# Two reciprocal roots of the Scan stage moved to GpSimd, and a group's sums and statistics spread over four rounds

## The reference

```
proj = hidden_states @ W_in.T                 # z (4096), xBC (4096 + 256), dt (64)
xBC  = silu(conv over 4 steps of xBC)         # x, B, C
dt   = softplus(dt + dt_bias)
y    = scan of x, B, C with decays exp(dt * A), + D * x
g    = y * silu(z)
gn   = g * rsqrt(mean(g * g) + 1e-5) * norm_w
out  = gn @ W_out.T                           # 4096 -> 256
```

## Time and profile before

| | us |
|---|---|
| median of 3 runs (3988.33 to 3993.56) | 3990.88 |
| the profiled execution | 3998.22 |
| its span | 3996.4 |
| TensorE busy in the span | 3464.1 (87%) |
| VectorE busy | 3056.8 (76%) |
| ScalarE busy | 1946.2 (49%) |
| GpSimd busy | 1167.3 (29%) |
| L3358, the taps, x408 | 302.4, 741 ns each |
| L3433, mE on GpSimd, x128 | 302.4, 2362 ns each |
| L3368, the scan, x128 | 297.1, 2321 ns each |

### The profile page before, as it was taken

The page is one execution under the profiler, slowest core; times in us unless marked ns, Lnnn a source line. Parts: engine busy times, 40 slices in busy tenths (PEclk is TensorE's granted clock), DMA queues, the critical chain, the costliest instruction groups (busy, mean ns, idle before and its releaser), DMA issues. The chain is left out here.

```text
span 3996.4 us, 65697 instructions
## 1 busy us (share of the span) xinstructions
PE 3464.1 (87%) x23619; PEld 2190.9 (55%) x23634; DVE 3056.8 (76%) x6556; ACT 1946.2 (49%) x4750; POOL 1167.3 (29%) x1208
## 2 busy tenths in 40 slices
PE   7799999999884485879899979889999999997875
PEld 3466666665553243654566655565655556564544
DVE  6799989989657766562477858869888888885678
ACT  4466666666553142421244434436655556563445
POOL 1533033306302100000011222106655555563210
PEclk9899999999997698989999989899999999997887
DMA  2222222222211100001000000311212222121000
GB/s 69 62 73 57 66 63 67 50 73 56 52 40 32 35 1 24 2 1 62 23 1 1 1 33 2 121 40 69 82 64 74 69 74 74 69 75 61 2 1 22
DMA packets 240529, 184.36 MB, mean 46 GB/s; under 512 B 117776, under 2 KB 216720, under 8 KB 239312
## 3 DMA queue, kind: packets, MB, share of 16 engines
q1 hardware_dynamic: 240208, 180.16, 15.0%
HBM read 164.88 MB, written 15.20 MB: 45 GB/s over the span
## 5 line engine op out<-in xcount | busy, mean ns | idle before, releaser
L310 PE MATMUL ps<-xT,min 128*128 128x512 f32 (+1 forms) x1072 | 505.1, 616 | 31.1 <-DVE macc L3358 30.8
L3358 DVE SCALAR_TENSOR_TENSOR macc<-ps,mcw,macc 128x508 f32<-128x508 f32 (+2 forms) x408 | 302.4, 741 | 82.7 <-ACT macc L3285 72.8
L3440 POOL TENSOR_TENSOR mSQ<-mSQ,mtn 128x512 f32<-128x512 f32 x128 | 239.9, 1874 | 365.7 <-ACT mtn L3310 365.6
L310 PEld LDWEIGHTS ps<-xT,min 128*128 128x128 f32 (+1 forms) x1072 | 192.3, 191 | 251.5 <-issue 204.8
L3433 POOL TENSOR_TENSOR mE<-mE,mCB 128x1024 f32<-128x1024 f32 x128 | 302.4, 2362 | 44.5 <-DVE mE L3368 26.5
L3368 DVE TENSOR_TENSOR_SCAN mE<-mE,mid 128x1024 f32<-128x1024 f32 x128 | 297.1, 2321 | 0.0
L3218 PE MATMUL ps<-mwo,macc 128*128 128x256 f32 x1024 | 245.0, 382 | 5.4 <-DVE macc L3375 5.4
L2946 ACT ACTIVATE hE<-ps 128x512 f32<-128x512 f32 x256 | 139.0, 595 | 220.9 <-PE ps L2908 220.9
L3306 ACT ACTIVATE mtn<-ps,mcol 128x64 f32<-128x64 f32 x1024 | 222.9, 334 | 3.0 <-PE ps L3197 2.8
L826 POOL TENSOR_TENSOR dTB<-did,dNB 128x1024 f32<-128x1024 f32 (+1 forms) x10 | 28.6, 2864 | 667.7 <-DMA dNB<-d_N 603.5
L2976 DVE TENSOR_REDUCE hMX<-ps 128x2 f32<-128x512 f32 x256 | 158.9, 684 | 60.0 <-PE ps L2887 60.0
(11 more groups left out here) (589 smaller groups left out, 8448.3 us busy)
## 6 DMA issues: line engine op xcount, KB each, us to landing
mE<-m_decay SPq DMA_DIRECT2D x128, 512.0 KB, 3.6
dwk<-in_L_attn_Wk SPq DMA_DIRECT2D x64, 128.0 KB, 2.3
dwq<-in_L_attn_Wq SPq DMA_DIRECT2D x64, 128.0 KB, 2.4
dwv<-in_L_attn_Wv SPq DMA_DIRECT2D x64, 128.0 KB, 2.4
dwg<-in_L_attn_Wg SPq DMA_DIRECT2D x64, 128.0 KB, 2.4
dwo<-in_L_attn_Wo SPq DMA_DIRECT2D x64, 128.0 KB, 2.7
min<-in_m_in SPq DMA_DIRECT2D x2, 4096.0 KB, 17.8
d_N<-dNT SPq DMA_DIRECT2D x256, 16.0 KB, 1.5
```

Source lines behind the costliest of these rows:

```text
L310: t = pe.matmul(out, w[:, j, :], self.c.xT[:, j, blk(g, 512)], start=j == 0, stop=j == 1)
L3358: x = dve.scalar_tensor_tensor(out=acc[:, :, 3 - j:T], in0=p[:, :, 0:T - 3 + j], scalar=self.cw[:, i, j:j + 1], in1=acc[:, :, 3 - j:T], op ...
L3440: pool.tensor_tensor(self.SQ[g % 2][:, :], self.SQ[g % 2][:, :], self.tn[s][:, :], ALU.add).then_inc(*self.sqa.up)
```

## The change

Both roots become a power with exponent -0.5 on GpSimd (`root_pool`); -0.5 stands in a constant of 128x4 in a spare column of `st`. The step "rsq" is now GpSimd's: it waits for `sw` and does one power. The step "rsqrt" is GpSimd's too: -mean, variance + 1e-5, the power, and the product. The one step "sums" becomes "sum0" to "sum3" with lags 7 to 10, and "stats" becomes "sta0" to "sta3" with lags 8 to 11 (the four aggregates go with "sta3"), one sum or statistic each. "rsqrt" and "scale" keep their lags 11 and 12, and "close" and "rsq" theirs. For the last group the steps stand together in three rounds of their own. The accumulator banks of a group come free with its last sum.

```
+    def root_pool(self, pool, own, out, var, eps, tmp):
+        if eps:
+            o = own(pool.tensor_scalar(tmp, var, eps, 1.0, ALU.add, ALU.mult))
+            pool.wait_ge(own.sem, o)
+        return pool.tensor_tensor(out, tmp, self.half, ALU.pow)
...
     def start_vector(self, dve, own):
         dve.memset(self.ones[:, :], 1.0)
+        dve.memset(self.half, -0.5)
...
-        for t in range(len(seq) + 13):
+        for t in range(len(seq) + 10):
...
-                            ("decay", t), ("rsq", t - 5), ("sums", t - 7), ("stats", t - 9), ("rsqrt", t - 11), ("scale", t - 12),
-                            ("tr", t - 1), ("taps", t), ("acc", t - 3), ("y", t - 2)):
+                            ("decay", t), ("rsq", t - 5), *self.ends(t), ("tr", t - 1), ("taps", t), ("acc", t - 3), ("y", t - 2)):
...
+    def ends(self, t):
+        last = len(self.seq) - 1
+        if t > last:
+            late = t - last
+            steps = {7: ("sum0", "sum1", "sum2", "sum3"), 8: ("sta0", "sta1", "sta2", "sta3", "rsqrt"), 9: ("scale",)}.get(late, ())
+            if steps:
+                return [(s, last) for s in steps]
+        steps = [(f"sum{j}", t - 7 - j) for j in range(4)] + [(f"sta{j}", t - 8 - j) for j in range(4)] + [("rsqrt", t - 11), ("scale", t - 12)]
+        return [(s, q) for s, q in steps if q < last]
...
-                    room[to] = room[to + 1] = self.summed.at(g + 1)
+                    room[to] = room[to + 1] = self.summed.at(4 * g + 4)
...
+            elif step[:3] == "sum":
+                j = int(step[3])
+                if j == 0:
+                    if g:
+                        dve.wait_ge(*c.xn.at(4 * self.n + g))
+                    dve.wait_ge(*self.accd.at(u + 1))
+                    dve.wait_ge(*self.rq.at(g + 1))
+                dve.scalar_tensor_tensor(out=c.R[:, j, :], in0=bank(to + j // 2)[:, blk(j % 2, 256)], scalar=self.sw[:, j:j + 1],
+                                         in1=c.X[:, 4 * g + j, :], op0=ALU.mult, op1=ALU.add).then_inc(*self.summed.up)
+            elif step[:3] == "sta":
+                j = int(step[3])
+                dve.wait_ge(*self.summed.at(4 * g + j + 1))
+                o = own(dve.bn_stats(c.st[:, j, 0:6], c.R[:, j, :]))
+                if j == 3:
+                    dve.wait_ge(own.sem, o)
+                    for k in range(4):
+                        x = dve.bn_aggr(c.st[:, k, 6:8], c.st[:, k, 0:6])
+                    x.then_inc(*self.var.up)
...
+            elif step == "rsq":
+                pool.wait_ge(*self.smv.at(g + 1))
+                c.root_pool(pool, own, self.sw[:, 0:4], None, 0, self.sw[:, 4:8]).then_inc(*self.rq.up)
+            elif step == "rsqrt":
+                flat = lambda k: c.st[:, :, k:k + 1].rearrange("p a b -> p (a b)")
+                pool.wait_ge(*self.var.at(g + 1))
+                pool.tensor_scalar(c.rsq[:, 12:16], flat(6), -1.0, 1.0, ALU.mult, ALU.mult)
+                o = own(c.root_pool(pool, own, c.rsq[:, 0:4], flat(7), 1e-5, c.pv))
+                pool.wait_ge(own.sem, o)
+                pool.tensor_tensor(c.rsq[:, 12:16], c.rsq[:, 12:16], c.rsq[:, 0:4], ALU.mult).then_inc(*self.off.up)
```

More of the change, by code:

```diff
@@ L84, in __init__ @@
         self.rsq = self.at("rsq", [128, 16], F32)
+        self.half, self.pv = self.st[:, :, 8:9].rearrange("p a b -> p (a b)"), self.rsq[:, 4:8]
         self.free0 = self.low
@@ L3108, in buffers @@
         self.dtx, self.sc, self.cols = v("dt_sum", 2), s("decay", 2), s("dt_cols", 2)
-        self.aexp, self.won, self.summed, self.smv, self.off = s("a", 2), p("wo", 2), v("summed", 4), v("mean", 4), v("offset", 4)
+        self.aexp, self.won, self.summed, self.smv, self.off = s("a", 2), p("wo", 2), v("summed", 16), v("mean", 4), p("offset", 4)
+        self.rq, self.var = p("rsqrt", 4), v("moments", 4)
         self.zm, self.xm, self.cbm, self.tr, self.y, self.accd, self.sm = (
@@ L3117, in ended @@
     def ended(self):
-        return self.summed.at(4)
+        return self.summed.at(16)
     def order(self):
         seq, units = self.seq, self.units_before
-        for t in range(len(seq) + 13):
+        for t in range(len(seq) + 10):
             for step, q in (("yd", t - 3), ("x2", t - 1), ("em", t - 1), ("z", t), ("sq", t - 3), ("x", t), ("close", t - 4), ("cb", t - 1),
-                            ("decay", t), ("rsq", t - 5), ("sums", t - 7), ("stats", t - 9), ("rsqrt", t - 11), ("scale", t - 12),
-                            ("tr", t - 1), ("taps", t), ("acc", t - 3), ("y", t - 2)):
+                            ("decay", t), ("rsq", t - 5), *self.ends(t), ("tr", t - 1), ("taps", t), ("acc", t - 3), ("y", t - 2)):
                 if not 0 <= q < len(seq):
@@ L3134, in order @@
                         yield step, q, units[q], g, i
-                elif step in ("close", "rsq", "sums", "stats", "rsqrt", "scale"):
+                elif step in ("close", "rsq", "rsqrt", "scale") or step[:3] in ("sum", "sta"):
                     if i == 31:
@@ L3378, in vector @@
                 dve.tensor_scalar(self.sw[:, 4:8], bank(6)[:, 0:4], 1.0 / 4096, 1e-5, ALU.mult, ALU.add).then_inc(*self.smv.up)
[L3379 to L3399, removed]
@@ L3401, in gpsimd @@
     def gpsimd(self, pool, own):
         c = self.c
+        pool.wait_ge(*c.const.at(1))
         pool.wait_ge(self.dma[0], 80)
```

## The result

The changed kernel takes 3958.92 us (median of 4 runs, 3955.16 to 3962.48), the kernel before 3989.61 in the runs beside it: 30.7 us less, a ratio of 0.9923 by the medians. The estimate of the ratio over the runs is 0.9917, with a 95% interval of 0.9903 to 0.9930, which is 28 to 39 us less. The forecast was 3957.8.

The account below looks back on a forecast made before the run. TensorE bounds Scan's rounds except at group ends, where late taps stall it. Loop -31.1 and tail -2.0 make -33.1 us: profiled 3998.2 becomes 3965.1, or 3957.8 with the 7.3 us distance to the median; likeliest case's range 3953 to 3963.

Parts of the forecast that it names:

- What stalls TensorE is the taps behind the roots: Scan's group ends: VectorE's roots, held by GpSimd, make the taps late for TensorE; moving both roots gives -31.1 us.
- Spreading is worth 0: VectorE in Scan: sums and statistics spread over rounds fit idle time and TensorE's slack, cost 0.
- P = 0.8 us: GpSimd at each root: assumed time of one 128x4 power, with bounds 0.258 and 2.36 us.
- The tail: 2.0 us less: Last group, all on the path: first root gains 1.3 us, second 0.7; bounds -3.1 to +1.1.
- Only the first power is long: Rival, GpSimd's first power: costs once what exceeds 3.6 us free; at 10 us +6, 3964; chance 0.06.
- The long-power rivals: GpSimd's powers at the roots: long ones cut the gain (5 us: 3978), chance 0.11, or make it slower, 0.03.
- 3 x (2P - 6.0) in the loop: Loop loss over three groups when long powers delay mE, the scan and the taps; 12.3 us at P = 5.
- ACT's scale: ACT's scale of a group waits for the second root, which GpSimd ends a round earlier: cost 0.
- The turning point: Power length on GpSimd at which loop and tail give back the 31.1 us gain: P = 6.6 us.
- the distance of 7.3 us between a profiled execution and the median: Whole kernel: the profiled execution stood 7.3 us above the runs' median 3990.9; the forecast took that distance along.

Follow-up runs that it names:

- e2: The changed kernel with both roots put back on VectorE, sums and statistics still spread: 3995.0 us, ratio 1.0013 to the kernel before.
- e8: The kernel before, with GpSimd's mSQ sum and mE product next to each root cut to 4 columns: 3964.4 us, ratio 0.9940.
- e4: The kernel before, with the one-source steps of Scan's two roots replaced by two-source ones: 3992.3 us, ratio 1.0005.
- e1: The changed kernel with the four sums back in one round and the four statistics in another: 3962.5 us, ratio 0.9928 to the kernel before.
- e9: The changed kernel with each power done seven times and ScalarE's scale of groups 0 to 2 two rounds later: 3973.8 us, ratio 0.9958 to before.
- e6: The changed kernel with each power done seven times in a row: 3989.5 us, ratio 1.0000 to the kernel before.
- e5: The changed kernel with each power done three times in a row: 3964.6 us, ratio 0.9940 to the kernel before.
- e3: The kernel before, with VectorE doing both roots behind the round's taps instead of ahead of them: 3964.2 us, ratio 0.9936.
- e5b: The changed kernel with each power done five times in a row: 3966.2 us, ratio 0.9945 to the kernel before.

## Why the prediction was right, step by step

- *What stalls TensorE is the taps behind the roots, 31.1 us in the loop.* Right: 31.05 us in the traces, none with the roots gone, all of it with the roots back (e2). That GpSimd holds the first steps is shown by e8 and by e4's end times. Of the loss, 18.5 us are TensorE's idle time (three times 3.27 + 2.90). Most of the rest is the clock: behind five of the six waits it is granted at 0.50, the lower of its two levels (1.2 GHz), for 3.41 us, and behind group 0's first for 6.83. That is 23.9 us at half speed, some 12.0 lost, and it is why group 0 lost 11.12 us and the others 9.98. With the waits gone, so are these.
- *Spreading is worth 0.* Right in the loop (e1, e2). In the tail it is 0.1 us, which the prediction hadn't priced.
- *P = 0.8 us.* Mis-sized: the eight powers take 1.01 to 1.04 us. The products around it cost 0.20 and not 0.26. mE is delayed by 1.0 and 1.9 us where 0.9 and 2.2 stood, and the taps by nothing.
- *The tail: 2.0 us less.* Right: 8.62 to 6.73, 1.9. Its parts came out a little differently: 1.1 for the first root where 1.3 stood (the longer power), 0.7 for the second (there the shorter small steps pay for it), and 0.1 in the sums and statistics between them, 3.39 us and not 3.51.
- *"Only the first power is long."* Didn't happen: group 0's first is 1.04 us. The Trainium skill (GPSIMD Engine Reference, section Instruction dispatch) states a cost for the first call of freshly loaded code. It isn't seen here: no idle time of GpSimd stands before that power.
- *The long-power rivals, 3 x (2P - 6.0) in the loop.* This formula failed in two places: it has no term for ACT's scale, which the prediction put at 0, and it lets mE's delay go to VectorE one to one. With five powers, meant as 5.4 us, the formula had 13 us in the loop and the run 2.7; with seven the sum of 38.5 against 36.0 measured (stretch 702.62 - 666.59) came near for the wrong reason, since 18.4 us of it went through ScalarE's scale and the clock behind it (e9). The turning point, 6.6 us of power by the formula, lies nearer to 7.5: e6's median equals that of the kernel before, its stretch is 3.1 us longer.
- *3957.8 against 3958.9.* That the two differ by only 1.1 us is in part luck: the four runs spread over 7.3 us, and the distance of 7.3 us between a profiled execution and the median, which the forecast took along, isn't there for the changed kernel, whose profiled execution, 3955.16, lies below its median. The stretch is the better test: 32.94 us less, forecast 33.1.

## What to carry to other kernels

A chain of tiny instructions on VectorE isn't priced by its count but by what GpSimd is running when it starts: here two of the first root's 11 steps made 5.2 us out of 2.1, where 1.9 us were free behind them. The waits then cost more than their own length, since TensorE's clock fell behind each: 31.05 us for 18.5 us of idle time. Look for such an instruction with many times its usual duration whose end coincides with the end of one on the other engine; moving it behind the step that TensorE waits for got five sixths of the loop's gain with no new code. When work is moved to a slower engine, price every reader of its result, not the queue behind it alone: the first to run out of slack was a third engine's step a round later.

## What the runs showed of the hardware that I had not expected

A power of 128x4 on GpSimd takes 1.02 us, five times its product or tensor-scalar of the same shape (0.20). The hold works in both directions and on tiny shapes: in e8 an mSQ sum of four columns took 1.43 us on GpSimd, starting at 3168.12 inside a scan that ended at 3169.55, and in e5 an mE product took 4.01 us for 2.36. TensorE's clock falls behind waits of either length, for a time that the transposes alone don't show. Behind group 1's wait of 2.90 us the transposes ran at 0.60 us and behind that of 3.27 at 1.06, but in both cases the granted clock was 0.50 for 3.41 us, from 3238.21 and from 3193.84. Behind the shorter wait these 3.41 us cover the x matmuls, which took 3.57 us where the same four for z, just before the wait, took 1.98:

```profile
3233.51 1.98 PE L310 MATMUL ps<-xT,min 128*128 128x512 f32 x4
```

Behind waits of 0.6 to 0.7 us (e3, e5b, e9) it stayed at 1.00, and with the idle time gone it is 1.00 throughout the stretch's loop.
